# Packing the score maxima of a causal attention kernel: one head pair per PSUM bank, or two for the short query blocks

## The reference

```python
h = x @ W1 + b1                       # q, k, v of 16 heads, 8 numbers each
w = einsum('bhqd,bhkd->bhqk', q, k) / sqrt(8)
w = softmax(w * mask - (1 - mask) * 1e6)      # causal: mask = tril(ones)
x = layernorm(x + (w @ v) @ Wp + bp)
# token-shift feed-forward: r = sigmoid(xr Wr'), k = relu(xk Wk')**2, x + r * (k Wv'), layernorm
```

## Time and profile before

| | |
|---|---|
| runs | 763.33, 766.25, 769.27 us, median 766.25 |
| profiled execution | 766.06 us, of which the span of the profile is 764.3 us |
| TensorE busy | 621.4 us (81% of the span) |
| VectorE busy | 557.7 us (73%), of which row maxima (L661) 401.3 us in 1024 instructions |
| ScalarE busy | 471.6 us (62%) |
| GpSimd busy | 378.4 us (50%) |
| mean granted TensorE clock | 0.959 of full speed |

### The profile page before, as it was taken

One profiled execution on the slowest core, in us unless ns is written; L12 is line 12 of the kernel. 1 busy time (PEld: TensorE's weight loads), 2 busy tenths in 40 slices (PEclk: granted clock), 3 DMA queues, 4 the chain that ended last, 5 costly groups with the idle time before them and its releaser, 6 DMA issues.

```text
span 764.3 us, 18024 instructions
## 1 busy us (share of the span) xinstructions
PE 621.4 (81%) x6733; PEld 279.5 (37%) x6733; DVE 557.7 (73%) x1644; ACT 471.6 (62%) x918; POOL 378.4 (50%) x520
## 2 busy tenths in 40 slices
PE   2256987998988989898989898988989898977743
PEld 2013233434343435343434434343435343433232
DVE  3067777778888887879797978788887978782231
ACT  1111676586767676677777686767676766677510
POOL 6110334355655655565556464655655565455533
PEclk9999999999999999999999999999999999999755
DMA  1241213132331323241413141332323231100100
GB/s 47 96 97 49 94 54 104 44 92 66 79 93 58 112 58 115 45 124 34 118 38 118 40 127 45 75 96 58 112 59 113 54 104 29 47 17 16 29 14 14
DMA packets 65500, 53.19 MB, mean 70 GB/s; under 512 B 10882, under 2 KB 61316, under 8 KB 65412
## 3 DMA queue, kind: packets, MB, share of 16 engines
q1 hardware_dynamic: 65412, 52.03, 24.5%
HBM read 34.70 MB, written 17.30 MB: 68 GB/s over the span
## 4 chain that ended last, share of the span: by engine, by line
PE 60%; DVE 21%; ACT 8%; issue 5%; POOL 2%; DMA 2%; SPq 1%; POOLq 0%; DVEq 0%; ACTq 0%
PE ops L510 15%; DVE rowmax L661 12%; PE sps L487 10%; PE tps L451 10%; PE spare L390 8%; ACT probs L592 6%; PE spare L404 5%; PE sps L472 3%; DVE h L714 3%; PE spare L430 2%; PE spare L417 2%; PE spare L420 1%; PE spare L402 1%; DVE y L703 1%; PE spare L427 1%
## 5 line engine op out<-in xcount | busy, mean ns | idle before, releaser
L661 DVE TENSOR_REDUCE rowmax<-sps 128x1 f32<-128x512 f32 (+7 forms) x1024 | 401.3, 448 | 103.0 <-PE sps L487 102.2
L592 ACT ACTIVATE probs<-tps 128x512 f32<-128x512 f32 x640 | 346.4, 595 | 149.9 <-PE tps L451 149.9
L761 POOL TENSOR_SCALAR_AFFINE_SELECT probs<-probs 128x512 f32<-128x512 f32 x256 | 158.0, 635 | 272.6 <-ACT probs L592 272.6
L510 PE MATMUL ops<-probs,vop 128*32 128x384 f32 (+3 forms) x2048 | 175.7, 450 | 5.5 <-POOL probs L761 4.2
L451 PE MATMUL tps<-qop,kop 50*128 50x384 bf16 (+3 forms) x1024 | 127.5, 307 | 39.9 <-ACT probs L592 36.1
L487 PE MATMUL sps<-kop,qop 48*64 48x512 bf16 (+7 forms) x2048 | 130.6, 310 | 11.9 <-DMA kop<-d_parts 11.9
L472 PE MATMUL sps<-qmask,dup 64*128 64x128 bf16 (+1 forms) x640 | 69.7, 215 | 38.2 <-DVE rowmax L661 34.0
L451 PEld LDWEIGHTS tps<-qop,kop 50*128 50x128 bf16 x1024 | 34.3, 94 | 164.2 <-ACT probs L592 111.5
L510 PEld LDWEIGHTS ops<-probs,vop 128*32 128x32 f32 x2048 | 50.5, 109 | 79.9 <-issue 61.2
L487 PEld LDWEIGHTS sps<-kop,qop 48*64 48x64 bf16 x2048 | 43.1, 106 | 54.5 <-issue 19.6
L472 PEld LDWEIGHTS sps<-qmask,dup 64*128 64x128 bf16 x640 | 31.4, 95 | 80.6 <-DVE rowmax L661 74.2
(11 more groups left out here) (70 smaller groups left out, 601.7 us busy)
## 6 DMA issues: line engine op xcount, KB each, us to landing
d_parts<-qk_parts SPq DMA_DIRECT2D x16, 768.0 KB, 3.8
qop<-d_parts SPq DMA_DIRECT2D x192, 32.0 KB
qop<-d_parts SPq DMA_DIRECT2D x64, 96.0 KB
kop<-d_parts SPq DMA_DIRECT2D x192, 32.0 KB
kop<-d_parts SPq DMA_DIRECT2D x64, 96.0 KB
xa<-L_attn_x SPq DMA_DIRECT2D x16, 256.0 KB, 3.0
xres<-L_attn_x SPq DMA_DIRECT2D x16, 256.0 KB, 3.4
out<-result SPq DMA_DIRECT2D x16, 256.0 KB, 2.5
```

Of the source, the lines that this page charges most:

```text
L510: last = nc.tensor.matmul(ops[32 * t:32 * t + 32, BLK * a:SEQ], vop[:, par, a, QUARTET * half + t, hh, :], probs[:, g % 2, i, off:off + w] ...
L592: nc.scalar.activation(probs[:, g % 2, i, :], tps[:, bank(4 * GROUPS * n + 4 * g + i), :], ACT.Exp, scale=SCALE)\
L661: last = nc.vector.reduce_max(rowmax[:, par, QUARTET * half + i, a:a + 1], sps[:, bank(n), off:off + w], axis=AX_X)
L761: last = nc.gpsimd.affine_select(out=v, in_=v, compare_op=ALU.is_ge, fill=0.0, base=0, pattern=[[0, QUARTET], [1, BLK]], channel_multiplie ...
```

## The change

`max_chunk` now takes the head pair i as well and says which head pairs share the bank. Groups c = 0 to 3 hold block 7, 6, 5 (with block 1 beside it) and 4 of one head pair. The short blocks 3, 2 and 0 move to c = 4, where head pairs i and i + 2 share a bank, side by side: banks 0 and 1 hold block 3 of two pairs (2 x 256 columns), banks 2 and 3 hold block 2 of two pairs (2 x 192) and block 0 of two pairs (2 x 64). Two pairs that lie side by side are reduced by one VectorE instruction with a two-row access pattern. For a batch entry that makes 52 maxima instructions in the place of 64, and 44 diagonal-mask matmuls in the place of 40; the score matmuls stay 128 with the same widths, in another order.

```diff
-def max_chunk(c):
-    wide = SEQ - QBLK * c
-    if c in (0, CHUNKS - 1):
-        return [(NQBLK - 1 - c, 0, wide)]
-    return [(NQBLK - 1 - c, 0, wide), (c - 1, wide, SEQ - wide)]
+def max_chunk(c, i):
+    one, two = (i,), (i % 2, i % 2 + 2)
+    if c == 4:
+        return [(3, 0, 4 * QBLK, two)] if i < 2 else [(2, 0, 3 * QBLK, two), (0, 6 * QBLK, QBLK, two)]
+    long = (7 - c, 0, SEQ - QBLK * c, one)
+    return [long, (1, 6 * QBLK, 2 * QBLK, one)] if c == 2 else [long]
...
 def s_masks(b, g, i):
...
-                    dst = sps[:, bank(n + k), :]
-                    if len(blocks) == 1:
-                        dst, src = dst[:, blocks[0][2] - QBLK:blocks[0][2]], qmask[r, 0, :]
+                    tile = sps[:, bank(n + k), :]
+                    if c == 2:
+                        diagonals = [tile[:, 4 * QBLK:].rearrange("p (j s) -> p j s", j=2)[:, :, QBLK:]]
                     else:
-                        apart = blocks[1][2]
-                        dst = dst[:, SEQ - 2 * apart:].rearrange("p (j s) -> p j s", j=2)[:, :, apart - QBLK:]
-                        src = qmask[r]
-                    nc.tensor.matmul(dst, dup[r, :], src, start=True, stop=False, skip_group_check=True)
+                        diagonals = [tile[:, off:off + len(pairs) * w].rearrange("p (j s) -> p j s", s=w)[:, :, w - QBLK:]
+                                     for _, off, w, pairs in max_chunk(c, i + k)]
+                    for j, dst in enumerate(diagonals):
+                        nc.tensor.matmul(dst, dup[r, :], qmask[r, 0:dst.shape[1], :], start=j == 0, stop=False,
+                                         skip_group_check=True)
...
 def s_chunks(b, par, g, i):
...
+                groups = [max_chunk(c, i), max_chunk(c, i + 1)]
+                blocks = [(j, m) for j, group in enumerate(groups[0]) for m in range(len(group[3]))]
+                for j, m in blocks:
                     for k in range(2):
-                        pair = QUARTET * half + i + k
+                        a, off, w, pairs = groups[k][j]
+                        pair = QUARTET * half + pairs[m]
...
 def reduce_chunk(b, par, g, i):
...
-                for a, off, w in max_chunk(c):
-                    last = nc.vector.reduce_max(rowmax[:, par, QUARTET * half + i, a:a + 1],
-                                                sps[:, bank(n), off:off + w], axis=AX_X)
+                for a, off, w, pairs in max_chunk(c, i):
+                    first = QUARTET * half + pairs[0]
+                    last = nc.vector.reduce_max(
+                        rowmax[:, par, first:first + 2 * len(pairs) - 1:2, a],
+                        sps[:, bank(n), off:off + len(pairs) * w].rearrange("p (j s) -> p j s", s=w), axis=AX_X)
```

More of the change, by code:

```diff
@@ L461, in s_masks @@
                 wait(pe, s_reduced, bank_free(n + 1))
-                blocks = max_chunk(c)
                 for k in range(2):
                     r = slice(HROWS * k, HROWS * k + QBLK)
-                    dst = sps[:, bank(n + k), :]
-                    if len(blocks) == 1:
-                        dst, src = dst[:, blocks[0][2] - QBLK:blocks[0][2]], qmask[r, 0, :]
-                    else:
-                        apart = blocks[1][2]
-                        dst = dst[:, SEQ - 2 * apart:].rearrange("p (j s) -> p j s", j=2)[:, :, apart - QBLK:]
-                        src = qmask[r]
-                    nc.tensor.matmul(dst, dup[r, :], src, start=True, stop=False, skip_group_check=True)
+                    tile = sps[:, bank(n + k), :]
+                    if c == 2:
+                        diagonals = [tile[:, 4 * QBLK:].rearrange("p (j s) -> p j s", j=2)[:, :, QBLK:]]
+                    else:
+                        diagonals = [tile[:, off:off + len(pairs) * w].rearrange("p (j s) -> p j s", s=w)[:, :, w - QBLK:]
[3 more added lines that the diff above has]
+                                         skip_group_check=True)
             def s_chunks(b, par, g, i):
@@ L479, in s_chunks @@
                     wait(pe, ops_in[half], LOADED * (before("S", b) + 1))
-                blocks = max_chunk(c)
-                for j, (a, off, w) in enumerate(blocks):
+                groups = [max_chunk(c, i), max_chunk(c, i + 1)]
+                blocks = [(j, m) for j, group in enumerate(groups[0]) for m in range(len(group[3]))]
+                for j, m in blocks:
                     for k in range(2):
-                        pair = QUARTET * half + i + k
+                        a, off, w, pairs = groups[k][j]
+                        pair = QUARTET * half + pairs[m]
                         for hh in range(2):
                             r = slice(HROWS * hh, HROWS * hh + TERMS)
-                            out = HROWS * half_of(i + k, hh)
-                            last = nc.tensor.matmul(sps[out:out + QBLK, bank(n + k), off:off + w],
+                            out = HROWS * half_of(pairs[m], hh)
+                            last = nc.tensor.matmul(sps[out:out + QBLK, bank(n + k), off + w * m:off + w * m + w],
                                                     qop[r, par, pair, QBLK * a:QBLK * a + QBLK],
                                                     kop[r, par, pair, 0:w], start=False,
-                                                    stop=j == len(blocks) - 1, skip_group_check=True)
-                        if j == len(blocks) - 1:
+                                                    stop=(j, m) == blocks[-1], skip_group_check=True)
+                        if (j, m) == blocks[-1]:
                             last.then_inc(s_done, 1)
```

## The result

The changed kernel is **slower**: 780.11 us median against 767.76 of the kernel before, both run again. The ratio is 1.0169 with a 95% interval of 1.0112 to 1.0225. A loss is clear of noise; whether it reaches 2% is open. The forecast was 775.5 (1.012), range 762 to 785. Medians in this document are over all executions of a kernel, while a ratio leaves out those that lie more than 1.5% above the fastest of the same kernel: here one of 2712 us (the other three have a median of 779.91), and further on four of the ten of after_both (the other six: 763.54). The profiled execution took 780.31 us with a span of 778.0, that is 13.7 us longer than the span before.

The account below looks back on a forecast made before the run. TensorE's order of work was taken to set the pace, with VectorE mattering where TensorE waits for maxima. Per step 0.51 + 0.38 - 0.26 = +0.63 us, times 15 = 9.5 us on 766.06: 775.5, own range 771 to 781, 8-in-10 range 762 to 785.

Parts of the forecast that it names:

- Groups 1 and 8: Shorter first banks: group 1 gains 0.26 us a step, group 8 gains 0.22 through shorter scores and masks on TensorE.
- Rival 4: Two-row maxima on VectorE cost as much as two instructions, so the change doesn't do what it says; chance 0.05.
- Group 6 does not keep it: Group 6's 0.26 us gain is lost because GpSimd holds `h` in group 7; taken as 0, ends 0 and 0.27.
- rival 1: Near no change: `h` slips one instruction ahead of GpSimd, or four blocks cost what two do; 764 to 772, chance 0.25.
- Group 9 runs into group 0: VectorE falls behind in group 9 and holds TensorE in group 0: +0.38 us a step, group 8's 0.22 gain included.
- group 4: Longer first maximum, four masks and sixteen score matmuls (taken as 0.45 us) delay TensorE by 0.51 us a step.
- rival 3: Much slower: TensorE's new pauses at groups 9 and 0 make the clock fall in every step; about 793, chance 0.08.
- a gain or loss per step counts 15 times: Stages S and T both run in 15 steps, so +0.63 us a step was multiplied by 15, giving 9.5 us.

Follow-up runs that it names:

- after_both: Changed kernel with `h` moved to group 6, z's moments to group 7 and `result` to group 8; 768.13 us, ratio 0.9958 to the kernel before.
- after_result8: Changed kernel with `result` (four VectorE instructions) moved from group 9 to group 8; 761.52 us, ratio 0.9944 to the kernel before.
- after_second_half: New packing for groups 5 to 9 alone, groups 0 to 4 as in the kernel before; one execution, 763.97 us.
- before_fill: Kernel before, with repeated transposed-score matmuls filling TensorE's wait in group 8; 763.45 us, ratio 0.9946.
- after_fill: Changed kernel with repeated transposed-score matmuls filling TensorE's wait in group 8; 768.32 us, ratio 1.0013 to the kernel before.
- after_swap: Changed kernel with `h` moved to group 6 and z's moments to group 7; 760.12 us, ratio 0.989 to the kernel before.

## Why the prediction was right, and where it was not

**Right: the direction and its mechanism.** The saved instructions were worth no more than where they stood. Groups 1 and 8 gained what the sum gave (0.24 and 0.19 us for 0.26 and 0.22), groups 2, 3 and 5 stayed, and groups 4, 9 and 0 lost more than that. That VectorE is too full in group 9 is shown by after_result8: with `result` taken out, 0.81 of 0.88 us come back. Rival 4 is out, as two rows cost 687 ns.

**Right sum, two wrong terms.** The step came out at +0.56 us for +0.63, but its terms were off by -0.31, +0.28 and -0.09, which nearly cancel: the sum was better than its parts, by luck. *"Group 6 does not keep it", for which I took 0*, was -0.31, past the end of 0.27 that I kept: `h` did slip one instruction ahead of GpSimd, as rival 1 described it, and groups 6 and 7 gave 0.31. *"Group 9 runs into group 0"*, +0.60 with group 8's gain left out, was +0.88: I had `result` at 1.10 us and did not ask what GpSimd does while I moved it 0.4 us on in group 9, though the earlier trace rows showed what it does to `h`. The mask there cost 0.33 of hold, which fits the 0.28 that the term lacked. Both errors are one: the held instruction was priced in the place where I saw it, and not where the change moves another one to. In group 4 the sixteen matmuls took 0.35 us, the lower bound, for 0.45: 0.42 for 0.51.

**Mis-sized: the clock, and the fifteen equal steps.** The sum left the falls as they were, and rival 3 had them in every step. In the traces they rose from three of 1.5 us to five of 3.0. The span's 13.7 us divide as: 12 steady steps x 0.56 = 6.7; falls in those steps 15.1 - 4.6 = 10.4; steps 1 and 2, 4.4 shorter; 1.0 after step 14. Of the 4.4, about 3 are a fall in step 2 that the trace before has and the trace after has not: groups 4 and 5 took 11.55 us there, and 8.48 in after_second_half, which packs them the same way and has no fall there. Another 0.9 stands in group 1 of step 1, which takes anything from 4.5 to 6.9 us in the traces with the new packing there, and is scatter. The windows from 75 to 155 us, before and then after:

```profile
75.00:155.00 80.00, 69.20 (x772) 27.61 (x770) 59.14 (x161) 53.34 (x104) 29.48 (x47) 0.98 0.24 72
```

```profile
75.00:155.00 80.00, 70.54 (x818) 28.67 (x818) 61.12 (x143) 56.53 (x111) 33.49 (x51) 1.00 0.25 78
```

So, by these traces, the packing costs some 7 us in the steps, where I summed 9.5. The step that failed is *"a gain or loss per step counts 15 times"*: steps 1 and 2, without the fall and the scatter, come out 0.4 us shorter together and not 1.3 longer. The steady step came 0.07 short as well. It costs another 7 us in falls, which I put at nothing. The two misses pull against each other: it is luck in part that the median ended only 4.6 us above the forecast, within its own range of 771 to 781. Without the new falls the change would lie inside the 8 us that I called no change.

That TensorE's rest in group 8 brings most falls in the kernel before is shown by before_fill; for the changed kernel after_fill says the same, by one trace and by a time 1.5% lower. In the changed kernel's trace steps 4 and 6 have one fall in group 0 and one in group 8, and steps 7, 10 and 13 one of twice the length, from group 8 into group 9. Why one step in several has a fall and its like do not, and how much of it the waits of group 0 do, stays open: after_swap had its falls there, after_second_half, with the same waits in group 0 and 1.27 in group 8, had one in group 8.

**What holds `h`.** The reading that a held instruction stands until GpSimd is through agrees with five places now (`h` at 1.80 and 1.93 us, `result` at 1.43, 1.87 and 2.12). In four others, where at most the tail of a GpSimd instruction overlaps the first of the four, they take 1.10 or 1.11. That fits what the Trainium skill says (SBUF — State Buffer, "SBUF: two separate sides"): VectorE and GpSimd share one pair of ports, the instruction that starts first keeps it to its end, and the other waits. It says so of VectorE instructions that use both of their ports; that these four do is not shown here. Not every GpSimd instruction holds them, though: `h`'s second one at 396.23 took 0.34 us in full beside L777, which ran from 396.18 to 396.47. Nor are the maxima, which read PSUM, held: the one at 405.32 took 0.55 us under the mask of 405.27. No run here removed GpSimd's work itself.

## What to carry to other kernels

Count a saved instruction at the queue place where it is saved, and then ask what the work that took its place pushes under whom: here 192 instructions less made the kernel 1.7% slower, about half of it through the clock. Taking four instructions a step out from under GpSimd, with the old packing, made it 2.0% faster (0.9722 to 0.988), the clock's part included. Where one engine's instruction is held by another's, price the hold at every place to which a change can shift it. Where TensorE must wait, matmuls in the wait that repeat what is there can be worth it (0.5% here), and a shorter wait more. And count falls of the clock apart from the steps: they differ from one execution to the next, and a forecast that leaves them out can be right for the wrong reason.

## What the runs showed of the hardware that I had not expected

A reduction with two output rows over 512 columns costs 687 ns, one row 682. Sixteen matmuls in four blocks of 192 and 64 columns hold TensorE for 0.35 us, as long as four of 512 (0.34): here the columns set the time, not the number of matmuls. The same four VectorE instructions took between 1.10 and 2.12 us, by what GpSimd did beside them. And falls of the clock cost a step 1.5 us or 3.0 us, as the granted clock over the step was 0.96 or 0.92, that is by once or twice the time at the lower level.
